# Side work of the attention in a new order, and maxima in two bf16 parts

## The chip, the cores and the metric

One core of one Trainium2 chip runs the whole program in one launch. The metric is the device time in microseconds (us).

## The reference, cut to what matters

The model is two layers on 16 sequences of 512 tokens with 256 features. Layer 0 is a gated convolution mixer and a recurrent network; layer 1 is causal attention and a mixture of experts with a fixed capacity. The change touches only the attention of layer 1:

```python
h = layernorm(x) * (1 + scale_a) + shift_a      # by sequence
q, k, v = split(h @ w_qkv, 3)                   # 16 heads of 16 features; q with a form of head_dirs, head_scales
s = q @ k.T                                     # causal, scaled
p = softmax(s)
x = x + gate_a * ((p @ v) @ w_out)
```

The program folds the scale and the form built from `head_dirs` and `head_scales` into the weight of q ahead of the loop.

## The kernel before, in words

The stages run one after the other: mixer, recurrent network, attention (`attention_stage`), router, choice of the tokens for each expert by counting, experts. The attention stage runs from about 1190 us to 2335 us of the span.

A batch is one sequence (NB = 16, `i` in the code). All five engines have a queue written out by hand, `pe_batch`, `dve_batch`, `act_batch`, the GpSimd block and `sp_batch`, with a loop over the middle batches and the first and last ones unrolled. They are tied by semaphores (`Signal`: `stp(b, k)` is the value after k steps of batch b). Each batch goes over 16 heads in four groups of 4.

**The main work of a head.** q and k are held as three bf16 parts each, in stacks of 96 rows (`q_stack`, `k_stack`), so that one matmul gives a product at nearly fp32 accuracy. `pe_max` (L1221) forms the scores with queries on partitions, seven heads ahead (AHEAD = 7); `dve_max` (L1450, the reduction is L1456) takes the maxima over keys. So head 9 of batch i forms the maxima of head 0 of batch i+1. After each fourth head, `pe_turn_max` (L1299) turns the maxima of the next group into a row, `dve_neg_max` (L1465) splits its negative into three bf16 parts, and `sp_row` (L1716) copies these into rows 96 to 98 of `q_stack`, where `k_stack` holds ones. `pe_scores` (L1240) then forms scores minus maximum with keys on partitions, contracting over 99 rows, `act_exp` (L1576) takes the exponential (L1586), and after four heads `pe_pv` (L1258) multiplies by the values; this product stands in heads 0, 4, 8 and 12. In each head the three fills f = 0, 1, 2 of scores and maxima alternate on TensorE. PSUM banks 0 to 2 hold scores, 3 and 4 maxima, 6 the values product, and 5 and 7 (`SIDE_A`, `SIDE_B`) all side work.

**The side work of batch i,** placed by head:

- head 0: values product of batch i (`pe_values`), kept by ScalarE (`act_values`)
- head 1: turn of the normalised x of batch i+1 (`pe_turn_ln`), then four ScalarE operations (`act_hT`) and two VectorE ones in head 2 (`dve_hT_lo`)
- heads 3 and 4: q and k products of batch i+1 (`pe_qk`, L1292), each of the four results copied to bf16 by ScalarE (`act_qk`, L1618), the rest formed by VectorE (`dve_qk_rest`, L1499), copied again (`act_qk2`, L1622), and the third part formed by GpSimd (`pool_qk3`, L1680)
- heads 2, 6, 9, 13: turns of the product with the values (`pe_turn_o`) and the division (`dve_normal`)
- heads 5, 7 and 8: output projection of batch i-1 (`pe_turn_tok`, `act_o_hi`, `dve_o_lo`, `pe_out`); heads 9 and 10: turning it back and adding it to x
- heads 8 and 11: statistics and normalisation of batch i+2.

**The queue of SyncE** carries all transfers, in the order of the code: `sp_row(i,1)`, `sp_store` of q and of k of batch i+1 to a DRAM buffer (12 transfers), `sp_row(i,2)`, `sp_load` of groups 0 and 1 of batch i+1 (6 transfers each, 768 KB), `sp_row(i,3)`, load 2, `sp_row(i+1,0)`, load 3. A load of group g waits for the scores of group g of batch i, the first one also for the stores:

```python
sp_row(sp, i, 2)
if not last:
    sp_load(sp, i + 1, 0)
    sp_load(sp, i + 1, 1)
```

Of the kernel before, what the change touches and what calls it, by code (L numbers as in the profile page):

```python
# [27 lines left out]
P = 128  # L28
# [1037 lines left out]
STACK = len(Q_PARTS) * HD  # L1066

# [76 lines left out]
def attention_stage(nc, t, ps, mem):  # L1144
# [7 lines left out]
    with ExitStack() as ctx:  # L1152
# [19 lines left out]
        var_eps, rstd = sb("var_eps", [P, TT]), sb("rstd", [P, TT])  # L1172
        xn = sb("xn", [P, TT, D])
# [5 lines left out]
        neg_top = sb("neg_top", [HEADS, 3, P], BF16)  # L1179
        neg_rest = sb("neg_rest", [HEADS, P])  # L1180
# [25 lines left out]
        lnt, hTf, hTh, hTl = signal("ln_turned"), signal("hT_full", DK), signal("hT_hi", DK), signal("hT_lo", DK)  # L1206
        vp, ve = signal("v_product", 2), signal("v_kept", 2)
# [4 lines left out]
        mtp, neg, row = signal("max_turned", NG), signal("neg_max", 4 * NG), [signal(f"max_row{g}", 48) for g in range(NG)]  # L1212
# [27 lines left out]
        def pe_scores(pe, b, h, f, first):  # L1240

            if h % GROUP == 0 and f == 0:
                pe.wait_ge(*row[h // GROUP](b, 48))

            if h:
                pe.wait_ge(*ex(b, 3 * (h - 1) + f + 1))
            elif not first:
                pe.wait_ge(*ex(b - 1, 3 * (HEADS - 1) + f + 1))
            for kt in ((0,), (1, 3), (2,))[f]:
                bk, col = ST_PLACE[kt]  # L1250
                w = T - kt * P
                pe.matmul(bank(bk)[:, col:col + w], k_stack[0:STACK + 3, h, kt * P:(kt + 1) * P],  # L1252
                          q_stack[0:STACK + 3, h, kt * P:T], start=True, stop=True)
                last = pe.matmul(bank(bk)[:, col:col + P], ident_b[:, :], mask_k[:, :],  # L1254
                                 start=False, stop=True, skip_group_check=True)
            last.then_inc(stp.sem, 1)

        def pe_pv(pe, b, g):  # L1258

            pe.wait_ge(*ex(b, 3 * GROUP * (g + 1)))  # L1260
            if g == 0:
                pe.wait_ge(*ve(b, 2))
# [21 lines left out]
        def pe_turn_ln(pe, b):  # L1284
            pe.wait_ge(*s_xn(b, TT))
            for f in range(DK):
                for n in range(TT):
                    last = pe.transpose(bank((SIDE_A, SIDE_B)[f])[:, n * P:(n + 1) * P], xn[:, n, f * P:(f + 1) * P],
                                        ident[:, :])
            last.then_inc(lnt.sem, 1)  # L1290
# [42 lines left out]
        def pe_batch(pe, i, first, last):  # L1333
            for h in range(HEADS):
                for f in range(3):
                    if f == 2 and h % GROUP == 0 and not (first and h == 0):
                        pe.wait_ge(*neg(i, 4 * (h // GROUP + 1)))
                        pe_pv(pe, *((i, h // GROUP - 1) if h else (i - 1, NG - 1)))
# [5 lines left out]
                if h % GROUP == 1 and not (last and h + GROUP > HEADS):  # L1344

                    g = h // GROUP
                    if g:
                        pe.wait_ge(*oe(i, g))
                    else:
                        pe.wait_ge(*(neg(i, 4) if first else oe(i - 1, NG)))  # L1350
                    pe_turn_max(pe, *((i, g + 1) if g + 1 < NG else (i + 1, 0)))
                if h == 0:
                    pe.wait_ge(*(qr(i, 4) if first else on(i - 1, 3)))
                    pe_values(pe, i)
                if h == 1 and not last:
                    pe.wait_ge(*ve(i, 2))
                    pe_turn_ln(pe, i + 1)
                if h == 2 and not first:
                    pe.wait_ge(*(ve(i, 2) if last else hTf(i + 1, 2)))
                    pe_turn_o(pe, i - 1, 3, SIDE_B)  # L1360
                if h == 3 and not last:
                    pe.wait_ge(*hTl(i + 1, DK))
                    pe_qk(pe, 0)
                    if not first:
                        pe.wait_ge(*on(i - 1, NG))
                    pe_qk(pe, 1)
                if h == 4 and not last:
                    for n in range(2):
                        pe.wait_ge(*qr(i + 1, n + 1))
                        pe_qk(pe, 2 + n)  # L1370
                if h == 5 and not first:
                    for f in range(DK):
                        pe.wait_ge(*(ve(i, 2) if last else qr(i + 1, 3 + f)))
                        pe_turn_tok(pe, i - 1, f)
                if h == 6:
                    pe.wait_ge(*(qr(i + 1, 4) if first else yl(i - 1, 2)))
                    pe_turn_o(pe, i, 0, SIDE_B)
                if h == 7 and not first:
# [9 lines left out]
                if h == 10 and not first:  # L1388
# [5 lines left out]
                if h == 14:  # L1394

                    pe.wait_ge(*(on(i, 1) if first else xs(i - 1, 2)))

        @block.tensor
        def _(pe):
            pe_turn_ln(pe, 0)  # L1400
# [3 lines left out]
            for n in range(2):  # L1404
                pe.wait_ge(*qr(0, n + 1))
                pe_qk(pe, 2 + n)
            for h in range(AHEAD):
# [4 lines left out]
            pe_batch(pe, 0, True, False)  # L1412
            with pe.Fori(1, NB - 1) as i:
                pe_batch(pe, i, False, False)
            pe_batch(pe, NB - 1, False, True)
# [25 lines left out]
        def dve_norm(dve, b, first=False):  # L1441
            if not first:
                dve.wait_ge(*lnt(b - 1, 1))
# [15 lines left out]
        def dve_hT_lo(dve, b):  # L1459
            for f in range(DK):  # L1460
                dve.wait_ge(*hTh(b, f + 1))
# [3 lines left out]
        def dve_neg_max(dve, b, g, first=False):  # L1465

            src, k = bank(PV_BANK)[0:HEADS, 0:P], 4 * g
            dve.wait_ge(*mtp(b, g + 1))
            if g or not (first or (isinstance(b, int) and b == 0)):

                dve.wait_ge(*(row[g - 1](b, 48) if g else row[NG - 1](b - 1, 48)))
# [41 lines left out]
        def dve_batch(dve, i, first, last, norm):  # L1513
            for h in range(HEADS):
                if h == 2 and not last:
                    dve_max(dve, i, h + AHEAD, (0, 1))
                    dve_hT_lo(dve, i + 1)
                    dve_max(dve, i, h + AHEAD, (2,))
# [7 lines left out]
                if h == 2 and not first:  # L1526
                    dve_normal(dve, i - 1, 3, SIDE_B)
                if h in (3, 4) and not last:
                    for n in range(2):
                        dve_qk_rest(dve, i + 1, 2 * (h - 3) + n)  # L1530
                if h == 5 and not first:
                    dve_o_lo(dve, i - 1)
                if h == 6:
                    dve_normal(dve, i, 0, SIDE_B)
                if h == 9:
# [3 lines left out]
                if h == 10 and not first:  # L1539
# [3 lines left out]
                if h == 11 and norm:  # L1543
# [5 lines left out]
        def _(dve):  # L1549
# [7 lines left out]
            dve.memset(k_stack[STACK:STACK + 3, :, :], 1.0).then_inc(const.sem, 1)  # L1557
            dve.memset(values[:, :, :, HD:HD + 1], 1.0).then_inc(const.sem, 1)
            dve.memset(values[:, :, :, HD + 1:], 0.0).then_inc(const.sem, 1)
            for h in range(AHEAD):  # L1560
# [33 lines left out]
        def act_values(act, b):  # L1594
            for n in range(2):
                act.wait_ge(*vp(b, n + 1))
                act.activation(values[:, 2 * n:2 * n + 2, :, 0:HD].rearrange("p a h c -> p a h c"),
                               bank((SIDE_A, SIDE_B)[n]).rearrange("p (a h c) -> p a h c", a=2, h=HEADS),
                               ACT.Copy).then_inc(ve.sem, 1)

        def act_hT(act, b):
            act.wait_ge(*lnt(b, 1))
            if not (isinstance(b, int) and b == 0):
                act.wait_ge(*q3(b - 1, 4))
            act.nop(nofuse=True)
            for f in range(DK):
# [3 lines left out]
            for f in range(DK):  # L1610
                act.wait_ge(*hTf(b, f + 1))
                act.activation(hT_s[0][:, f, :], hT[:, f, :], ACT.Copy).then_inc(hTh.sem, 1)

        def act_qk(act, b, n):
            act.wait_ge(*qp(b, n + 1))
            if n == 0 and not (isinstance(b, int) and b == 0):
                act.wait_ge(*stored(b - 1, 32))
# [17 lines left out]
        def act_batch(act, i, first, last):  # L1635
            for h in range(HEADS):
# [3 lines left out]
                if h == 0:  # L1640
                    act_values(act, i)
                if h == 1 and not last:
                    act_hT(act, i + 1)
                if h in (3, 4) and not last:
# [6 lines left out]
                if h in (7, 8) and not first:  # L1651
                    act_delta(act, i - 1, h - 7)

        @block.scalar
        def _(act):
# [6 lines left out]
            act_batch(act, 0, True, False)  # L1662
            with act.Fori(1, NB - 1) as i:
                act_batch(act, i, False, False)
            act_batch(act, NB - 1, False, True)
# [16 lines left out]

        @block.gpsimd
        def _(pool):
# [3 lines left out]
            with pool.Fori(0, NB - 2) as i:  # L1688
                pool_qk3(pool, i + 1)
                pool_rstd(pool, i + 2)  # L1690
            pool_qk3(pool, NB - 1)

# [23 lines left out]
        def sp_row(sp, b, g):  # L1716
            sp.wait_ge(*neg(b, 4 * (g + 1)))
            for j in range(3):
# [861 lines left out]
```

## Time and profile before

| | us |
|---|---|
| median of 3 runs | 2859.42 (2857.22 to 2860.83) |
| the profiled execution, its own time | 2858.73 |
| its span, first to last instruction | 2856.9 |
| TensorE busy | 2382.5 |
| VectorE busy | 1555.3 |
| ScalarE busy | 1290.6 |
| GpSimd busy | 503.2 |
| mean granted TensorE clock | 0.924 of full |

Busy time is summed over the whole span, with stages of different limits. PE is TensorE's matmul queue, PEld its weight loads, DVE VectorE, ACT ScalarE, POOL GpSimd, SP SyncE; a `q` behind a name marks the engine's sequencer. Matmuls overlap and their ends are modelled, so starts are the safer reading. A granted clock of 1.00 is 2.4 GHz and 0.50 is 1.2 GHz. An arrow `<-` behind an idle time names what ended it.

### The profile page before, as it was taken

The numbers are of one execution on the slowest core, as the hardware profiler recorded it, in microseconds if no ns is written. First come the engines' busy times: TensorE is split into PE (matmuls) and PEld (weight loads), VectorE is DVE, ScalarE is ACT, GpSimd is POOL, SyncE is SP. The second block draws the span as 40 slices with busy tenths as digits, with TensorE's granted clock in tenths as the row PEclk, the third lists the DMA queues.
The fourth block names the chain that finished last, engine by engine and source line by source line (L and its number), as shares of the span: only waits on it lengthen the run. The fifth ranks groups of instructions, "written<-read, shape, count | busy, mean of one in ns | idle before, by whom it ended". The sixth has DMA issues, their size and how long they took to land. (4 is left out here: it accounts for less than half of the span.)

```text
span 2856.9 us, 46003 instructions
## 1 busy us (share of the span) xinstructions
PE 2382.5 (83%) x15266; PEld 1797.4 (63%) x15266; DVE 1555.3 (54%) x3568; ACT 1290.6 (45%) x2197; POOL 503.2 (18%) x413
## 2 busy tenths in 40 slices
PE   7999999999699998557888788888888878149997
PEld 6777777777478886435555555555555548139996
DVE  4444444444344443456666666666666556666664
ACT  2444444444355555524555455555555545014442
POOL 0111111111011113400000000000000003026663
PEclk8999999999899999769999999999999989569999
DMA  3200000000100000022233222222222206535542
GB/s 118 77 0 0 0 0 0 0 0 0 30 0 0 0 0 22 24 75 75 69 73 74 70 70 68 67 69 74 69 67 72 71 3 236 157 108 112 124 91 38
DMA packets 123435, 157.38 MB, mean 55 GB/s; under 512 B 26848, under 2 KB 104048, under 8 KB 123248
## 3 DMA queue, kind: packets, MB, share of 16 engines
q1 hardware_dynamic: 109040, 131.17, 16.6%
q0 software_dynamic: 14336, 25.44, 4.6%
q8 instruction: 35, 0.57, 0.1%
q14 instruction: 24, 0.20, 0.0%
HBM read 96.78 MB, written 58.98 MB: 55 GB/s over the span
## 5 line engine op out<-in xcount | busy, mean ns | idle before, releaser
L1456 DVE TENSOR_REDUCE at_top<-psum 128x1 f32<-128x512 f32 (+3 forms) x1024 | 448.0, 484 | 334.7 <-PE psum L1236 331.8
L1586 ACT ACTIVATE at_probs<-psum 128x512 f32<-128x512 f32 (+1 forms) x768 | 372.1, 530 | 407.5 <-PE psum L1254 405.2
L1234 PE MATMUL psum<-at_k_stack,at_q_stack 96*128 96x512 bf16 (+3 forms) x1024 | 299.7, 319 | 167.0 <-DMA at_k_stack<-qk_parts 116.9
L1252 PE MATMUL psum<-at_q_stack,at_k_stack 99*128 99x512 bf16 (+3 forms) x1024 | 293.0, 313 | 40.8 <-DMA at_q_stack<-at_neg_top 24.2
L1234 PEld LDWEIGHTS psum<-at_k_stack,at_q_stack 96*128 96x128 bf16 x1024 | 104.4, 102 | 271.2 <-issue 100.4
L1236 PE MATMUL psum<-at_mask_q,at_ident_b 128*128 128x128 bf16 x1024 | 208.1, 229 | 0.0
L1254 PE MATMUL psum<-at_mask_k,at_ident_b 128*128 128x128 bf16 x1024 | 204.7, 226 | 0.0
L1252 PEld LDWEIGHTS psum<-at_q_stack,at_k_stack 99*128 99x128 bf16 x1024 | 103.8, 101 | 135.8 <-issue 62.1
L1680 POOL TENSOR_TENSOR at_q_parts<-at_hT,at_q_parts 128x512 bf16<-128x512 f32 x32 | 36.6, 1165 | 681.3 <-ACT at_q_parts L1622 681.3
L1270 PE MATMUL psum<-at_probs,at_values 128*32 128x512 f32 (+3 forms) x2048 | 151.8, 437 | 0.9 <-ACT at_probs L1586 0.9
L570 POOL TENSOR_TENSOR y<-y,mean 128x512 f32<-128x512 f32 x64 | 83.3, 1330 | 366.0 <-ACT mean L623 366.0
L2288 POOL DMA_INDIRECT out<-ex_result,slot_tokens x64 | 119.9, 1874 | 101.9 <-DVE ex_result L2420 87.3
L613 ACT ACTIVATE y_hi<-y 128x512 fp32r<-128x512 f32 x64 | 40.5, 632 | 164.6 <-DVE y L491 164.6
L2466 ACT ACTIVATE ex_mid<-psum,ex_b_up 128x512 f32<-128x512 f32 x96 | 66.2, 689 | 107.0 <-PE psum L61 103.6
L1270 PEld LDWEIGHTS psum<-at_probs,at_values 128*32 128x32 f32 x2048 | 60.1, 110 | 82.4 <-issue 63.7
L59 PE MATMUL psum<-ex_w_down_hi,ex_mid_hi 128*128 128x256 f32 x384 | 109.0, 284 | 1.4 <-DVE ex_mid_lo L2399 1.4
L61 PE MATMUL psum<-ex_w_down_hi,ex_mid_lo 128*128 128x256 f32 x384 | 107.5, 280 | 0.0
L60 PE MATMUL psum<-ex_w_down_lo,ex_mid_hi 128*128 128x256 f32 x384 | 107.5, 280 | 0.0
L1254 PEld LDWEIGHTS psum<-at_mask_k,at_ident_b 128*128 128x128 bf16 x1024 | 104.2, 102 | 1.8
L1236 PEld LDWEIGHTS psum<-at_mask_q,at_ident_b 128*128 128x128 bf16 x1024 | 105.1, 103 | 0.0
L59 PE MATMUL psum<-hT_hi,w_in_hi 128*128 128x512 f32 x256 | 102.0, 398 | 3.5 <-DVE hT_lo L426 3.5
L59 PE MATMUL psum<-h_hi,w_conv_hi 128*128 128x512 f32 x256 | 102.4, 400 | 0.0
(405 smaller groups left out, 6215.1 us busy)
## 6 DMA issues: line engine op xcount, KB each, us to landing
qk_parts<-at_q_parts SPq DMA_DIRECT2D x96, 128.0 KB
qk_parts<-at_k_parts SPq DMA_DIRECT2D x96, 128.0 KB
at_q_stack<-qk_parts SPq DMA_DIRECT2D x64, 192.0 KB
at_k_stack<-qk_parts SPq DMA_DIRECT2D x64, 192.0 KB
x_residual<-in_x SPq DMA_DIRECT2D x16, 512.0 KB, 8.5
at_q_stack<-qk_parts SPq DMA_DIRECT2D x64, 128.0 KB
at_k_stack<-qk_parts SPq DMA_DIRECT2D x64, 128.0 KB
token_rows<-ro_h_tok SPq DMA_DIRECT2D x16, 512.0 KB, 3.1
```

The source lines that it names most:

```text
L59: pe.matmul(out, w[0], x[0], start=start, stop=False)
L60: pe.matmul(out, w[0], x[1], start=False, stop=False)
L61: return pe.matmul(out, w[1], x[0], start=False, stop=stop)
L570: pool.tensor_tensor(dev[:, m, :], y[:, m, :], mean[:, :], ALU.subtract).then_inc(dv.sem, 1)
L1234: pe.matmul(out, q_stack[0:STACK, h, qt * P:(qt + 1) * P], k_stack[0:STACK, h, 0:w], start=True, stop=True)
L1236: last = pe.matmul(bank(MAX0 + n % 2)[:, col + w - P:col + w], ident_b[:, :], mask_q[:, :], start=False, stop=True, skip_group_check=True)
L1252: pe.matmul(bank(bk)[:, col:col + w], k_stack[0:STACK + 3, h, kt * P:(kt + 1) * P], q_stack[0:STACK + 3, h, kt * P:T], start=True, stop=True)
L1254: last = pe.matmul(bank(bk)[:, col:col + P], ident_b[:, :], mask_k[:, :], start=False, stop=True, skip_group_check=True)
L1270: last = pe.matmul(bank(PV_BANK)[32 * hh:32 * hh + 32, kt * P:T], values[:, kt, GROUP * g + hh, :], probs[:, slot(GROUP * g + hh), P_COL[k ...
L1456: dve.tensor_reduce(top[:, h, qt:qt + 1], bank(MAX0 + n % 2)[:, col:col + w], AX.X, ALU.max).then_inc(mxr.sem, 1)
L1586: act.activation(probs[:, slot(h), 512 * f:512 * f + w], bank(f)[:, 0:w], ACT.Exp).then_inc(ex.sem, 1)
L2288: pool.indirect_dma_start(out=rows_out, out_offset=bass.IndirectOffsetOnAxis(ap=index[:, e, c * TT + a:c * TT + a + 1], axis=0), in_=resul ...
```

## The change

- The maxima are split into two bf16 parts instead of three (`N_SHIFT = 2`): two VectorE operations and one of the three row transfers per group are gone, and the scores contract over 98 rows.
- The q and k products of batch i+1 and all that follows from them stand in heads 0 and 1.
- The turn of the normalised x is for batch i+2, one half in head 13 and the other in head 14, half f = 1 first; ScalarE's four operations stand in head 14, VectorE's two in head 15.
- The values product is that of batch i+1, in head 3. ScalarE keeps it as it lies in a new tile `v_tok`, and GpSimd copies that into `values`, 32 columns a head (`pool_values`).
- Turns and divisions of the product with the values are in heads 4, 7, 10 and 13; the output projection in heads 5 to 9, with its second product behind head 9 instead of head 8; its way back in heads 10 and 11; the normalisation in head 12.
- Ahead of batch 0 the values of batch 0 and the normalised x of batch 1 are made as well. One more batch (the last but one) is unrolled on TensorE, ScalarE and GpSimd.
- The queue of SyncE keeps its order.

```diff
+N_SHIFT = 2
...
-        neg_top = sb("neg_top", [HEADS, 3, P], BF16)
-        neg_rest = sb("neg_rest", [HEADS, P])
+        neg_top = sb("neg_top", [HEADS, N_SHIFT, P], BF16)
...
+                if h in (0, 1) and not last:
+                    for n in (2 * h, 2 * h + 1):
+                        if n == 0:
+                            pe.wait_ge(*hTl(i + 1, DK))
+                        elif n >= 2:
+                            pe.wait_ge(*qr(i + 1, n - 1))
+                        pe_qk(pe, n)
+                if h == 3 and not last:
+                    pe.wait_ge(*qr(i + 1, 4))
+                    pe_values(pe, i + 1)
+                if h == 4 and not first:
+                    if not last:
+                        pe.wait_ge(*ve(i + 1, 2))
                     pe_turn_o(pe, i - 1, 3, SIDE_B)
-                if h == 3 and not last:
-                    pe.wait_ge(*hTl(i + 1, DK))
-                    pe_qk(pe, 0)
...
-                if h == 8 and not first:
-                    pe.wait_ge(*on(i, 1))
-                    pe_out(pe, i - 1, 1)
                 if h == 9:
-                    pe.wait_ge(*(qr(i + 1, 3) if first else dl(i - 1, 1)))
+                    if not first:
+                        pe.wait_ge(*on(i, 1))
+                        pe_out(pe, i - 1, 1)
...
                 if h == 13:
                     pe.wait_ge(*on(i, 2))
                     pe_turn_o(pe, i, 2, SIDE_A)
...
+                    if turn:
+                        pe.wait_ge(*(on(i, 1) if first else xs(i - 1, 2)))
+                        pe_turn_ln(pe, i + 2, 1)
+                if h == 14 and turn:
+                    pe.wait_ge(*on(i, 3))
+                    pe_turn_ln(pe, i + 2, 0)
...
             dve.wait_ge(*neg(b, k + 1))
-            dve.scalar_tensor_tensor(neg_rest[:, :], src, -1.0, neg_top[:, 0, :], ALU.mult,
+            dve.scalar_tensor_tensor(neg_top[:, 1, :], src, -1.0, neg_top[:, 0, :], ALU.mult,
                                      ALU.subtract).then_inc(neg.sem, 1)
-            dve.wait_ge(*neg(b, k + 2))
-            dve.tensor_copy(neg_top[:, 1, :], neg_rest[:, :]).then_inc(neg.sem, 1)
-            dve.wait_ge(*neg(b, k + 3))
-            dve.tensor_tensor(neg_top[:, 2, :], neg_rest[:, :], neg_top[:, 1, :], ALU.subtract).then_inc(neg.sem, 1)
...
+                if h in (0, 1) and not last:
+                    for n in range(2):
+                        dve_qk_rest(dve, i + 1, 2 * h + n)
+                if h == 4 and not first:
                     dve_normal(dve, i - 1, 3, SIDE_B)
...
-                if h == 5 and not first:
+                if h == 6 and not first:
                     dve_o_lo(dve, i - 1)
...
+                if h in (0, 1) and not last:
                     for n in range(2):
-                        act_qk(act, i + 1, 2 * (h - 3) + n)
+                        act_qk(act, i + 1, 2 * h + n)
                     for n in range(2):
-                        act_qk2(act, i + 1, 2 * (h - 3) + n)
-                if h == 5 and not first:
+                        act_qk2(act, i + 1, 2 * h + n)
+                if h == 3 and not last:
+                    act_values(act, i + 1)
+                if h == 6 and not first:
                     act_o_hi(act, i - 1)
...
+                if h == 14 and turn:
+                    act_hT(act, i + 2)
...
+        def pool_values(pool, b):
+            pool.wait_ge(*ve(b, 2))
+            if isinstance(b, int) and b == 0:
+                pool.wait_ge(const.sem, 3)
+            else:
+                pool.wait_ge(*pv(b - 1, NG))
+            pool.nop(nofuse=True)
+            pool.tensor_copy(values[:, :, :, 0:HD], v_tok[:, :, :].rearrange("p a (h c) -> p a h c", h=HEADS)
+                             ).then_inc(vs.sem, 1)
...
         def sp_row(sp, b, g):
-            sp.wait_ge(*neg(b, 4 * (g + 1)))
-            for j in range(3):
+            sp.wait_ge(*neg(b, N_SHIFT * (g + 1)))
+            for j in range(N_SHIFT):
```

## Rows read from the trace of the kernel before

**Rows 1.** The page, part 1: busy us, share of the span, instructions.
```profile
PE 2382.5 (83%) x15266; PEld 1797.4 (63%) x15266; DVE 1555.3 (54%) x3568; ACT 1290.6 (45%) x2197; POOL 503.2 (18%) x413
```

**Rows 2.** Windows: stretch, its us, busy us by engine, granted clock, DMA share, GB/s.
```profile
1390.01:1458.56 68.55, 56.86 (x488) 37.36 (x489) 43.00 (x112) 35.23 (x70) 5.56 (x5) 0.95 0.27 70
1436.70:1443.50 6.80, 5.26 (x26) 3.96 (x27) 3.78 (x11) 1.12 (x3) 0.00 (x0) 0.50 0.14 57
1290.00:1293.40 3.40, 3.40 (x20) 1.53 (x22) 1.45 (x3) 1.19 (x2) 0.00 (x0) 0.50 0.24 75
...
1452.00:1457.00 5.00, 3.95 (x37) 2.54 (x36) 4.86 (x14) 3.12 (x8) 0.00 (x0) 1.00 0.28 60
1457.00:1459.00 2.00, 1.76 (x17) 1.06 (x16) 1.79 (x5) 1.23 (x3) 0.00 (x0) 1.00 0.01 2
```

**Rows 3.** TensorE's waits, 1325 to 2277 us: us in total, times, longest.
```profile
PE psum L1234 <- DMA at_k_stack<-qk_parts: 86.2, 14, 6.7
PE psum L1234 <- DVE at_top L1456: 40.4, 57, 1.0
PE psum L1252 <- DMA at_q_stack<-at_neg_top: 15.2, 15, 1.4
PE psum L1252 <- ACT at_probs L1586: 15.0, 26, 0.9
```

**Rows 4.** Timeline of TensorE in one batch: start, us, instruction, idle before it.
```profile
1408.12 0.39 PE L1252 MATMUL psum<-at_q_stack,at_k_stack 99*128 99x512 bf16 x1
...
1409.46 2.36 PE L1270 MATMUL psum<-at_probs,at_values 128*32 128x512 f32 x32
1412.07 0.48 PE L59 MATMUL psum<-at_hT_hi,at_wk_hi 128*128 128x512 f32 x1
...
1414.95 0.39 PE L1252 MATMUL psum<-at_q_stack,at_k_stack 99*128 99x512 bf16 x1
...
1426.38 0.39 PE L1252 MATMUL psum<-at_q_stack,at_k_stack 99*128 99x512 bf16 x1 [1.39 <-DMA at_q_stack<-at_neg_top]
...
1431.79 0.39 PE L1252 MATMUL psum<-at_q_stack,at_k_stack 99*128 99x512 bf16 x1
...
1438.24 0.61 PE L1234 MATMUL psum<-at_k_stack,at_q_stack 96*128 96x512 bf16 x1 [6.00 <-DMA at_k_stack<-qk_parts]
```

**Rows 5.** Timeline of SyncE, which issues the transfers, same batch.
```profile
1418.63 3.63 SPq L1701 DMA_DIRECT2D qk_parts<-at_k_parts  x6
1422.38 1.83 SPq L1719 DMA_DIRECT2D at_q_stack<-at_neg_top  x3
1425.75 1.97 SPq L1713 DMA_DIRECT2D at_q_stack<-qk_parts  x3
...
1429.31 1.85 SPq L1713 DMA_DIRECT2D at_q_stack<-qk_parts  x3
...
1446.79 1.92 SPq L1713 DMA_DIRECT2D at_q_stack<-qk_parts  x3
```

**Rows 6.** Timeline of VectorE: a rest, and pieces two and four of the maxima.
```profile
1414.38 0.69 DVE L1499 TENSOR_TENSOR at_hT<-psum,at_k_parts 128x512 f32<-128x512 f32 x1 [1.65 <-ACT at_k_parts L1618]
...
1418.28 0.28 DVE L1474 SCALAR_TENSOR_TENSOR at_neg_rest<-psum,at_neg_top 16x128 f32<-16x128 f32 x1
...
1418.84 0.28 DVE L1479 TENSOR_TENSOR at_neg_top<-at_neg_rest,at_neg_top 16x128 bf16<-16x128 f32 x1
```

**Rows 7.** Timeline of TensorE in batch 0: the waits for a transfer.
```profile
1289.71 0.39 PE L1252 MATMUL psum<-at_q_stack,at_k_stack 99*128 99x512 bf16 x1 [3.38 <-DMA at_q_stack<-at_neg_top]
1301.47 0.61 PE L1234 MATMUL psum<-at_k_stack,at_q_stack 96*128 96x512 bf16 x1 [5.76 <-DMA at_k_stack<-qk_parts]
```

**Rows 8.** Groups of GpSimd, 1190 to 2330 us: busy us, mean ns, idle before.
```profile
L1680 POOL TENSOR_TENSOR at_q_parts<-at_hT,at_q_parts 128x512 bf16<-128x512 f32 x32 | 36.6, 1165 | 681.3 <-ACT at_q_parts L1622 681.3
```

**Rows 9.** Groups of ScalarE, same stretch and columns.
```profile
L1618 ACT ACTIVATE at_k_parts<-psum 128x512 bf16<-128x512 f32 x32 | 19.1, 597 | 24.2 <-PE psum L61 24.2
```

More of the change, by code:

```diff
@@ L1211, in attention_stage @@
         mxp, mxr = signal("max_scores", 3 * HEADS), signal("max", 4 * HEADS)
-        mtp, neg, row = signal("max_turned", NG), signal("neg_max", 4 * NG), [signal(f"max_row{g}", 48) for g in range(NG)]
+        mtp, neg, row = signal("max_turned", NG), signal("neg_max", N_SHIFT * NG), [signal(f"max_row{g}", 16 * N_SHIFT) for g in range(NG)]
         stp, ex = signal("scores", 3 * HEADS), signal("exp", 3 * HEADS)
@@ L1282, in pe_values, with pe_turn_ln @@
                 last.then_inc(vp.sem, 1)
-        def pe_turn_ln(pe, b):
+        def pe_turn_ln(pe, b, f):
             pe.wait_ge(*s_xn(b, TT))
[L1286 to L1289, printed above, removed]
+            for n in range(TT):
+                last = pe.transpose(bank((SIDE_A, SIDE_B)[f])[:, n * P:(n + 1) * P], xn[:, n, f * P:(f + 1) * P],
+                                    ident[:, :])
             last.then_inc(lnt.sem, 1)
@@ L1330, in pe_turn_delta, with pe_batch @@
             last.then_inc(hp.sem, 1)
-        def pe_batch(pe, i, first, last):
+        def pe_batch(pe, i, first, last, turn):
             for h in range(HEADS):
@@ L1349, in pe_batch @@
                     else:
-                        pe.wait_ge(*(neg(i, 4) if first else oe(i - 1, NG)))
+                        pe.wait_ge(*(neg(i, N_SHIFT) if first else oe(i - 1, NG)))
                     pe_turn_max(pe, *((i, g + 1) if g + 1 < NG else (i + 1, 0)))
[L1352 to L1357, printed above, removed]
@@ L1385, in pe_batch @@
+                if h == 10:
+                    pe.wait_ge(*(ve(i + 1, 2) if first else dl(i - 1, 1)))
                     pe_turn_o(pe, i, 1, SIDE_A)
@@ L1387, in pe_batch @@
                         pe_turn_delta(pe, i - 1, 0)
-                if h == 10 and not first:
+                if h == 11 and not first:
                     pe.wait_ge(*xs(i - 1, 1))
@@ L1459, in dve_hT_lo @@
         def dve_hT_lo(dve, b):
-            for f in range(DK):
-                dve.wait_ge(*hTh(b, f + 1))
+            for k, f in enumerate((1, 0)):
+                dve.wait_ge(*hTh(b, k + 1))
                 dve.tensor_tensor(hT_s[1][:, f, :], hT[:, f, :], hT_s[0][:, f, :].bitcast(F32),
@@ L1514, in dve_batch @@
             for h in range(HEADS):
[L1515 to L1518, printed above, removed]
+                if h == 15 and norm:
+                    dve_max(dve, i + 1, h + AHEAD - HEADS, (0, 1))
+                    dve_hT_lo(dve, i + 2)
+                    dve_max(dve, i + 1, h + AHEAD - HEADS, (2,))
                 elif h + AHEAD < HEADS:
@@ L1538, in dve_batch @@
                         dve_add(dve, i - 1, 0)
-                if h == 10 and not first:
+                if h == 11 and not first:
                     dve_add(dve, i - 1, 1)
@@ L1609, in act_hT @@
                                scale=mod[:, SCALE_A + f, bass.ds(b, 1)]).then_inc(hTf.sem, 1)
-            for f in range(DK):
-                act.wait_ge(*hTf(b, f + 1))
+            for k, f in enumerate((1, 0)):
+                act.wait_ge(*hTf(b, k + 1))
+                if k == 0 and not (isinstance(b, int) and b == 0):
+                    act.wait_ge(*vp(b - 1, 2))
                 act.activation(hT_s[0][:, f, :], hT[:, f, :], ACT.Copy).then_inc(hTh.sem, 1)
@@ L1633, in act_delta, with act_batch @@
                            scale=mod[:, GATE_A + m, bass.ds(b, 1)]).then_inc(dl.sem, 1)
-        def act_batch(act, i, first, last):
+        def act_batch(act, i, first, last, turn):
             for h in range(HEADS):
@@ L1661, in _ @@
                     act_qk2(act, 0, 2 * m + n)
[L1662 to L1665, printed above, removed]
+            act_values(act, 0)
+            act_hT(act, 1)
+            act_batch(act, 0, True, False, True)
+            with act.Fori(1, NB - 2) as i:
+                act_batch(act, i, False, False, True)
+            act_batch(act, NB - 2, False, False, False)
+            act_batch(act, NB - 1, False, True, False)
             b = NB - 1
```

105 lines of the change are left out of this document (50 added, 55 removed).

## The prediction

> **What bounds the kernel now.** I began with the page's engine totals: TensorE is busy 83% of the span and no other engine over 54% [rows 1]. The page's chain that ended last stays in the last stage, so it says nothing about attention. I therefore took one steady batch of the attention by itself, from the first score product of one batch to that of the next: 68.55 us, TensorE busy 56.86, VectorE 43.00, ScalarE 35.23, GpSimd 5.56 [rows 2]. So TensorE sets the pace and is idle 11.7 us a batch. The list of TensorE's waits over the 14 steady batches (1 to 14) says for what [rows 3]: 86.2/14 = 6.16 us a batch for the loads of the next batch's q and k stacks, 15.2/14 = 1.09 us for the row of negated maxima, 40.4/14 = 2.89 us for the maxima on VectorE, 15.0/14 = 1.07 us for the exponentials on ScalarE. In the timeline of the batch that starts at 1390 the big wait stands in one place: 6.00 us before the first maximum of the next batch, in head 9, and 1.39 us of row wait before head 8 [rows 4]. Right behind the big wait the granted clock is 0.50, the 1.2 GHz level, for 6.8 us [rows 2].
>
> The timeline of SyncE shows why the loads are late [rows 5]. The store of k is issued from 1418.63 to 1422.26, then the three row transfers, then load 0 at 1425.75, and load 1 at 1429.31. TensorE gets load 0 at 1438.24, 12.5 us after its first issue [rows 4, 5]. The queue runs in the order of the code: sp_row(i,1), two stores, sp_row(i,2), loads 0 and 1. The row was ready when VectorE ended its fourth piece at 1419.12 [rows 6], but queued behind the store.
>
> **The change part by part.** I count heads by their first score product: head 5 starts at 1414.95, head 8 at 1426.38 after its wait, head 9 at 1431.79 [rows 4].
>
> *Row wait.* The q and k products move from heads 3 and 4 to heads 0 and 1, three heads earlier. The stores then end before head 5's maxima are turned. The row for head 8 is no longer behind them: it is ready at head 5 + 3.6 us (below) and lands some 2 us after issue (head 5 + 7), whereas head 8 starts at head 5 + 10. The 1.09 us goes.
>
> *Load wait.* Load 0 still stands behind sp_row(i,2), which needs the maxima of head 5. So it moves forward only to: second VectorE piece ended at 1418.28 + 0.28 = 1418.56, head 5 + 3.6 [rows 6]; two row issues instead of three, 2 x 0.61 = 1.2 [rows 5]; 0.2 for hand-over (estimate). First load issue at head 5 + 5.0, against + 10.8 before. Do the stores hold it up? The k store's last issue was at 1422.26 and load 0 started 3.5 us later, at 1425.75, the moment the store had landed [rows 5]: head 4 + 17.6, with head 4 at 1408.12 [rows 4]. The new head 1 has no probabilities-by-values product in it (about 2 us; 2.36 with its modelled end [rows 4]), so k has landed at about head 1 + 15.6, and head 5 + 5.0 is head 1 + 21. There are 5 us to spare.
>
> When does it land? Load 1 follows at once, since it only waits for the scores of head 7; so the nearest row is the 12.5 us of the same pair: head 5 + 17.5. When does TensorE want it? Head 9 came 16.84 us after head 5. Off go 1.39 of row wait and one output product, which moves behind head 9: 12 such matmuls took from 1412.07 to 1414.95, so 6 take 1.4 [rows 4]. That leaves 14.05, and 0.45 for the first scores: head 5 + 14.5. New wait 3.0 us; gain 6.16 - 3.0 = 3.2. The bound below: load 2 alone, issued at 1446.79, has no traffic left after 1457 [rows 2, 5], 10.2 us, which makes the wait 0.6. The bound above is the present 6.2.
>
> The Trainium skill, page "DMA: Bandwidth & Descriptors", section "Rules for kernel authors", says that a copy whose outermost dimension is a broadcast of c copies uses at most c of the 16 DMA engines; the loads of q repeat a part 3 and 2 times that way. This trace agrees: a load's tail runs at a DMA share of 0.28 and 0.14 [rows 2]. By that rule two loads in a row share the same few engines and the second one lengthens the first, which speaks against rival B and for the 12.5 us: 2780 by the rule, 2733 without it.
>
> *Clock.* After the 6 us wait the engine does 5.26 us of busy work at 0.50 [rows 2]; at full clock that is half, so 2.6 us a batch are lost. The only gap near 3 us in this stage that began at full clock, 3.38 us before 1289.71, was followed by a stretch of 3.40 us at 0.50 [rows 2, 7], which costs 1.7. The new gap is a little shorter and its place in time will vary, so I take half of that, 0.85, and a gain of 1.8. Bounds: 0 (nothing gained) to 2.6.
> The Trainium skill, "TensorE: Matmul & The Clock Gate", section "What's actually happening", says the clock follows how busy the engine has recently been. By that rule a gap left in head 9 can still drop the clock and give 0 here; rival C prices this from the rows.
>
> *New small waits.* Now 4.0 us a batch go on waits for VectorE and ScalarE, for the most part just behind the q and k side work, which queues in front of maxima and exponentials [rows 3]. Before, the second half of it sat in head 4 with its values product, about 2 us of TensorE work that hides the chain ScalarE copy, VectorE rest, ScalarE copy. Head 1 has none. VectorE can't take head 1's maxima until two 0.6 us copies and 0.69 us rests of head 0 are done [rows 6, 9], about 1.3 us into head 1, so TensorE waits some 0.9 at its third fill; the same in head 2 and at head 3's first exponential (0.9 together); ScalarE's four operations on the normalised x now stand between the exponentials of heads 14 and 15 (1.1, as now in head 2); the o_lo pair moves to the bare head 6 and holds the maxima of head 7 (1.4); 0.7 stays in heads 10 and 11. Sum 5.0. The two VectorE pieces fewer are off the path except in the load's chain, counted above. I take +1.1 net. Bounds: -1 (all in slack) to +11, rival D. The places are read from the code's order, the sizes are estimates from these durations.
>
> *Costed at nothing.* GpSimd's new spreading copy of the values: its subtraction over 512 elements takes 1.16 us [rows 8], so 1024 elements take some 2.3 us; it starts after head 0's values product and GpSimd next has work 4 us later. Cover gone, it delays q's third part and the stores, which have 5 us to spare. The score product contracts over 98 rows instead of 99: same duration by columns. ScalarE's copy of the values keeps its size. More code (one more unrolled batch): nothing in the trace prices it; I take 0, up to 10 us in all.
>
> *Sum of a steady batch:* -1.1 -3.2 -1.8 +1.1 = -5.0 us; times 14 = -70.
>
> *Batch 0 and the start.* Batch 0 waited 3.38 and 5.76 us [rows 7]. It has no output product or token turn between heads 5 and 9 (1.4 + 0.85), so its new load wait is 3.0 + 2.25 = 5.3: gain 3.9. Its clock drop shortens by 1.7, the new waits cost 1.1: about -4. Before it, the first values product (24 matmuls of half width, 2.8 us) and the last batches' turn (0.9) fall into the first load's long wait or away, and the wait for the first row loses two VectorE pieces and one issue, 1.1: about -5.
>
> Total -79 us. The profiled span is 2856.9 and its own time 2858.7, 0.7 under the median; 2856.9 - 79 = 2778, plus 1.8 = 2780.
>
> **The rivals.**
> *A, as above:* load wait about 3 us: 2780, own range 2765 to 2800. Chance 0.48.
> *B, the load comes in time:* it takes 10.2 us, the wait is 0.6, and the clock doesn't fall: -1.1 -5.6 -2.6 +1.1 = -8.2, x14 = -115, less 11 at the start: 2733. For it: load 2 alone. Against: load 1 is issued right behind. 0.20.
> *C, the wait shrinks but the clock falls all the same:* -1.1 -3.2 +1.1 = -3.2, x14 = -45, -9: 2805. For it: the 3.38 us gap that dropped the clock. 0.17. In its extreme the small waits take up the load wait's gain as well and the change gives nothing measurable (2859): 0.05.
> *D, slower:* the side work stops TensorE in heads without a values product. Ceiling, with nothing overlapped: 16 ScalarE operations of 0.60 (9.6) and 8 VectorE ones of 0.69 (5.5) are 15.1 us of waits against 4.0 [rows 3, 6, 9]: +11.1 -6.1 = +5.0 a batch, x14 = +70, -9: 2920. It decides from waits of about 10.7 us a batch on. Against: today the same chains cost 4.0. 0.10.
>
> **How the numbers follow.** A and most of B and C hold 0.85; the range 2730 to 2835 leaves out D, the no-gain case and a little of B. About 0.2% (6 us) is what a measurement here can tell from no change. Faster 0.85, same 0.05, slower 0.10.
>
> **What would show it.** The steady period falls from 68.3 to about 63.3. The wait on the row before head 8 is gone. Load 0's first issue comes 5 us after head 5, no longer right behind a store, and the wait in head 9 is 2.5 to 3.5 us. The 0.50 stretches are shorter or fewer. TensorE's waits for maxima and exponentials rise to about 5 us a batch, in heads 1, 2 and 7. Wrong would be: a load wait under 1 us or near 6, waits over 8 us in the bare heads, or rows that still queue behind stores.

## The result, and the profile after

The changed kernel takes 2777.48 us, the median of 4 runs (2776.81 to 2780.32), against 2858.38 for the kernel before in 4 runs: a ratio of 0.972, 95% interval 0.9706 to 0.9735. The forecast was 2780, range 2730 to 2835. The profiled span went from 2856.9 to 2778.2 us, 78.7 less, of which 76.4 lie in the attention stage.

TensorE's waits over batches 1 to 14, the list that answers to [rows 3]; us in total, times, longest:

```profile
PE psum L1235 <- DMA at_k_stack<-qk_parts: 47.2, 14, 3.9
PE psum L1235 <- DVE at_top L1461: 46.3, 70, 1.0
PE psum L1253 <- ACT at_probs L1588: 15.7, 27, 1.1
PE psum L1253 <- DMA at_q_stack<-at_neg_top: 0.8, 2, 0.6
```

The load wait (the first line; the view names the transfer of a load that was issued last) is 47.2/14 = 3.37 us a batch instead of 6.16, the row wait 0.06 instead of 1.09. The waits for maxima and exponentials rose from 3.96 to 4.43.

One steady batch and the stretch behind its load wait, as windows (columns as in [rows 2]):

```profile
1442.57:1507.05 64.48, 56.56 (x488) 37.36 (x489) 41.03 (x104) 34.73 (x71) 6.60 (x6) 0.95 0.31 74
...
1483.50:1489.90 6.40, 6.36 (x26) 4.17 (x27) 2.24 (x6) 1.74 (x4) 0.00 (x0) 0.50 0.11 44
```

The same batch on TensorE: heads 5 and 9, and the end of the load wait, as in [rows 4]:

```profile
1466.55 0.38 PE L1253 MATMUL psum<-at_q_stack,at_k_stack 98*128 98x512 bf16 x1
...
1479.92 0.39 PE L1253 MATMUL psum<-at_q_stack,at_k_stack 98*128 98x512 bf16 x1
...
1483.54 0.61 PE L1235 MATMUL psum<-at_k_stack,at_q_stack 96*128 96x512 bf16 x1 [3.17 <-DMA at_k_stack<-qk_parts]
```

SyncE in that batch, as in [rows 5]:

```profile
1458.52 3.88 SPq L1725 DMA_DIRECT2D qk_parts<-at_k_parts  x6
1469.67 1.21 SPq L1743 DMA_DIRECT2D at_q_stack<-at_neg_top  x2
1471.08 1.97 SPq L1737 DMA_DIRECT2D at_q_stack<-qk_parts  x3
...
1474.62 1.85 SPq L1737 DMA_DIRECT2D at_q_stack<-qk_parts  x3
```

The k store is issued by 1462.4, and SyncE then stands still until the row of head 5's maxima is ready at 1469.67. Load 0 starts at 1471.08, head 5 + 4.5 us (it was + 10.5), and TensorE has it at 1483.54, 12.5 us later. The order of the queue is now what holds the load back, where before it was the store: by the traces' semaphore events the last transfer of the store had landed 0.02 us before load 0 was issued in the kernel before, and 5.1 us before it in the changed one (batches 2 to 4). The clock still falls: to 0.50 for 3.4 or 6.8 us in 13 of the 14 batches.

### The profile page after: what moved, and what is told of

Same layout as the page of the kernel before. It is cut to its first block and busy times, and to the rows that moved or that the text cites. A ratio compares the mean times of both kernels' runs of the same rounds, so it can differ in the third digit from the quotient of the medians.

```text
span 2778.2 us, 45597 instructions
## 1 busy us (share of the span) xinstructions
PE 2366.8 (85%) x15266; PEld 1791.3 (64%) x15266; DVE 1525.3 (55%) x3440; ACT 1282.9 (46%) x2197; POOL 518.5 (19%) x429
## 5 line engine op out<-in xcount | busy, mean ns | idle before, releaser
L1588 ACT ACTIVATE at_probs<-psum 128x512 f32<-128x512 f32 (+1 forms) x768 | 365.8, 530 | 346.5 <-PE psum L1255 344.5
L1253 PE MATMUL psum<-at_q_stack,at_k_stack 98*128 98x512 bf16 (+3 forms) x1024 | 288.9, 309 | 23.1 <-ACT at_probs L1588 16.8
L1253 PEld LDWEIGHTS psum<-at_q_stack,at_k_stack 98*128 98x128 bf16 x1024 | 102.5, 100 | 115.1 <-issue 44.2
L61 PE MATMUL psum<-hT_hi,w_in_lo 128*128 128x512 f32 x256 | 102.0, 398 | 0.0
```

The lines of the kernel that those rows point to most:

```text
L61: return pe.matmul(out, w[1], x[0], start=False, stop=stop)
L1253: pe.matmul(bank(bk)[:, col:col + w], k_stack[0:STACK + N_SHIFT, h, kt * P:(kt + 1) * P], q_stack[0:STACK + N_SHIFT, h, kt * P:T], start=T ...
L1588: act.activation(probs[:, slot(h), 512 * f:512 * f + w], bank(f)[:, 0:w], ACT.Exp).then_inc(ex.sem, 1)
```

## The experiments

Every run is timed against the kernel before on the same chip. Unless its diff says otherwise it starts from the changed kernel. "First use" is the matmul that ends or would end the load wait; means over batches 2 to 12, and the period over batches 1 to 13, all worked out from the traces:

| run | us | ratio (95%) | period | load 0 issued, after head 5 | issue to first use | load wait |
|---|---|---|---|---|---|---|
| before | 2858 | | 68.36 | 10.46 | 12.66 | 6.13 |
| changed | 2777.5 | 0.972 (0.9706-0.9735) | 63.69 | 4.53 | 12.56 | 3.28 |
| e1 load first | 2799.1 | 0.979 (0.9777-0.9810) | 64.85 | -0.36 | no wait | 0 |
| e2 two parts alone | 2849.5 | 0.997 (0.9956-0.9981) | 68.10 | 10.46 | 12.70 | 6.38 |
| e3 three parts | 2804.3 | 0.982 (0.9799-0.9831) | 65.33 | 5.72 | 12.63 | 4.54 |
| e4 load 1 later | 2804.0 | 0.981 (0.9791-0.9824) | 65.30 | 4.53 | 11.13 | 1.85 |
| e5 row from ScalarE | 2781.6 | 0.974 (0.9719-0.9752) | 63.92 | -0.54 | no wait | 0 |
| e6 the same, before | 2857.1 | 1.000 (0.9990-1.0009) | 68.42 | 10.50 | 12.61 | 7.34 |
| e7 single loads | 2691.7 | 0.942 (0.9406-0.9437) | 58.61 | 4.53 | no wait | 0 |
| e8 single, first | 2698.6 | 0.945 (0.9429-0.9461) | 58.76 | -0.43 | no wait | 0 |
| e9 single, before | 2754.8 | 0.964 (0.9622-0.9654) | 62.01 | 10.48 | 7.41 | 0.90 |
| e10 cut by heads | 2732.1 | 0.956 (0.9542-0.9574) | 60.61 | 4.53 | 10.94 | 1.65 |
| e11 single, three parts | 2704.9 | 0.946 (0.9445-0.9476) | 59.16 | 5.72 | no wait | 0 |

**Which half of the change did it: e2 and e3.** e2 gives the kernel before the two parts alone:

```diff
-            dve.scalar_tensor_tensor(neg_rest[:, :], src, -1.0, neg_top[:, 0, :], ALU.mult,
+            dve.scalar_tensor_tensor(neg_top[:, 1, :], src, -1.0, neg_top[:, 0, :], ALU.mult,
                                      ALU.subtract).then_inc(neg.sem, 1)
-            dve.wait_ge(*neg(b, k + 2))
-            dve.tensor_copy(neg_top[:, 1, :], neg_rest[:, :]).then_inc(neg.sem, 1)
-            dve.wait_ge(*neg(b, k + 3))
-            dve.tensor_tensor(neg_top[:, 2, :], neg_rest[:, :], neg_top[:, 1, :], ALU.subtract).then_inc(neg.sem, 1)
...
-            for j in range(3):
+            for j in range(2):
```

> The kernel before, with the maxima in two parts and nothing else changed. Theory (before, load 0 started when the stores had landed, so a shorter row does not move it): load 0 still starts at head 4 + 17.6 us, the row wait of head 8 shrinks by up to 0.6 us and the load wait of head 9 grows by as much; the time is within 3 us of before. Rival (the two parts carry a share of the gain by themselves): 10 us or more faster.

It came out 8.7 us faster, more than the 3 expected and less than the rival's 10. The steady period fell by only 0.26 us, 3.4 over 13 batches; the attention stage as a whole took 4.8 us less, and 3.8 of the difference between the two profiled executions lies ahead of the stage, in code that is the same. The place of load 0 did not move.

e3 starts from the changed kernel and makes the maxima three parts again.

> The changed kernel, with the maxima in three parts again. Theory (in the new order load 0 does stand behind the row): two VectorE pieces and one issue, together 1.2 us, are back ahead of load 0, its wait goes from 3.4 to about 4.5 us, the low stretches of the clock are 6.8 us in nearly every batch, the steady period is about 65.3 us and the time about 2801 us. Rival (the order alone gave everything): 2778 us.

As forecast in three points: 1.19 us later issue, load wait 4.54, 2804 us. The fourth was missed: the low stretches of the clock are 3.4 us in 10 of the 14 batches and 6.8 in only four, so a longer wait did not make the clock dearer. The order alone is worth 54 us, the two parts alone at most 9, and together they give 81, so the two parts are worth 27 us in the new order. Of the 1.64 us a batch that they save there, 1.2 are load wait, since they stand in front of the late load; the rest is nearly all waits for maxima, 0.5 of them in head 14.

**Is it the place in the queue: e1, e5 and e6.** e1:

```diff
-            sp_row(sp, i, 2)
             if not last:
                 sp_load(sp, i + 1, 0)
+            sp_row(sp, i, 2)
+            if not last:
                 sp_load(sp, i + 1, 1)
```

> The changed kernel, with load 0 of the next batch put ahead of the row transfers of group 2 in the queue of SyncE. Theory (what is left of the load wait is load 0 standing behind the row, which needs the maxima of head 5): load 0 starts when the k store has landed, about 0.8 us before head 5 instead of 4.5 us after it, lands 12.5 us later, before head 9 asks for it; the 3.4 us wait goes, the granted clock stays at 1.00 through the batch, the steady period falls from 63.6 to about 59 us and the kernel to about 2711 us. Rival (the load is held by the transfers themselves, and gets longer or starts no sooner): a wait of 2 us or more stays in head 9 and the time stays above 2750 us.

A miss: 22 us slower than the changed kernel. The load wait did go. TensorE at head 8 and then SyncE in one batch of this run:

```profile
1547.84 0.61 PE L1253 MATMUL psum<-at_q_stack,at_k_stack 98*128 98x512 bf16 x1 [4.14 <-DMA at_q_stack<-at_neg_top]
```

```profile
1534.86 1.94 SPq L1737 DMA_DIRECT2D at_q_stack<-qk_parts  x3
1536.85 1.34 SPq L1737 DMA_DIRECT2D at_k_stack<-qk_parts  x3
1538.70 1.21 SPq L1743 DMA_DIRECT2D at_q_stack<-at_neg_top  x2
```

Load 0 starts before head 5 as forecast, and the row is issued only a little late, at 1538.70. But the scores of head 8 wait for it until 1547.84: 9 us for 8 KB, in two transfers of 4 KB. The row wait is 56.4/14 = 4.03 us a batch, more than the 3.37 of load wait that went. The view of that line has all four rows of a batch together: typical 1.7 us, the longest 8.6. The two transfers of this row took 3.8 to 4.3 and 7.5 to 8.6 us.

```profile
DMA to landing us min/median/max: 1.7/1.7/8.6
```

So neither theory held as it was put: the wait changed its object. e5 tries the row on another queue (load 0 ahead of it as in e1, `sp_row(sp, i, 2)` gone):

```diff
+        def act_row(act, b, g):
+            act.wait_ge(*neg(b, N_SHIFT * (g + 1)))
+            for j in range(N_SHIFT):
+                act.dma_start(q_stack[STACK + j:STACK + j + 1, GROUP * g:GROUP * (g + 1), :].rearrange(
+                    "a h (q p) -> a (h q) p", p=P), neg_top[:, j, :]).then_inc(row[g].sem, 16)
...
+                if h == 6:
+                    act_row(act, i, 2)
```

> The changed kernel, with load 0 as soon as the k store has landed, and the row transfers of group 2 issued by ScalarE in head 6, on a queue of their own. Theory (in the run with load 0 ahead of the row, the row of 8 KB sat 4 to 8 us behind the load's data in the same queue): from its own queue it lands about 2 us after its issue, head 8 waits under 1 us, the load wait of head 9 is gone and the clock stays at 1.00: steady period about 59.3 us, time about 2716 us. Rival (the row waits for the load's data on the transfer engines, whatever queue it comes from): 3 to 4 us of wait stay in head 8 and the time stays near 2799 us.

Its own queue did not free the row. Landing times of that line:

```profile
DMA to landing us min/median/max: 2.2/4.1/6.3
```

The row wait of head 8 fell to 20.3/13 = 1.56 us, but ScalarE is held for the issues, the two o_hi operations come later and with them VectorE's o_lo, and head 7 waits 2.0 us for maxima instead of 0.9. In the end the run is 4 us over the changed kernel, although its listed waits are 0.7 us a batch shorter (7.2 against 7.9). The difference is the clock, which the theory had at 1.00: behind the waits in heads 7 and 8 it fell in all 14 batches, for 6.8 us in 10 of them. A window inside such a stretch:

```profile
1545.00:1548.00 3.00, 3.00 (x19) 1.10 (x21) 1.14 (x3) 0.60 (x1) 0.00 (x0) 0.50 0.13 52
```

The rival was right on the mechanism, a wait on the transfer engines whatever queue, and wrong on the size.

e6 is the same edit (three parts, no change of the loads) on the kernel before:

> The kernel before, with the row transfers of group 2 issued by ScalarE in head 6 and nothing else changed. Theory (before, load 0 waited for the stores of the products of heads 3 and 4, not for the row): load 0 still starts at head 4 + 17.6 us; the row wait of head 8 shrinks, the load wait of head 9 grows by as much, and the time is within 5 us of 2858. Rival (it was the row in the queue that held up the loads before, too): 20 us or more faster.

Ratio 1.000. The row wait is gone (1.4 us in all in the list, against 15.2 before) and the load wait grew from 6.13 to 7.34. Load 0 is still issued at head 5 + 10.5 with no row in front of it: before, it was the store alone that held it.

**Why a load takes 12.5 us: e4, e7, e10.** e4 puts `sp_load(sp, i + 1, 1)` behind `sp_row(sp, i, 3)`.

> The changed kernel, with load 1 moved behind the row of group 3, so that load 0 has the transfer engines to itself. Theory (the second load lengthens the first): TensorE gets load 0 about 10 us after its first issue instead of 12.5, the wait in head 9 falls to about 1 us and the clock stays up there; but load 1 is then late for head 13 and about as much is lost there. Rival (a load takes 12.5 us by itself): the wait in head 9 stays at 3.4 us, and the wait in head 13 comes on top.

Issue to use fell to 11.1 us, not 10; the wait in head 9 to 1.85; and 3.9 us of wait appeared in head 13, where load 1 is wanted. So the second load costs the first one 1.4 us. The clock did not stay up as expected, it fell in every batch, and the run is 26 us slower than the changed kernel. e7 cuts the loads:

```diff
-                sp.dma_start((q_stack, k_stack)[side][n[0] * HD:n[1] * HD, GROUP * g:GROUP * (g + 1), :], src
-                             ).then_inc(loaded[g].sem, 16)
+                for s in range(n[1] - n[0]):
+                    sp.dma_start((q_stack, k_stack)[side][(n[0] + s) * HD:(n[0] + s + 1) * HD,
+                                                          GROUP * g:GROUP * (g + 1), :], src[s]
+                                 ).then_inc(loaded[g].sem, 16)
...
-        loaded = [signal(f"loaded{g}", 16 * len(LOADS)) for g in range(NG)]
+        loaded = [signal(f"loaded{g}", 16 * sum(n[1] - n[0] for _, n, _ in LOADS)) for g in range(NG)]
```

> The changed kernel, with each load of a group cut into 12 transfers of one part each (16 partitions, 64 KB) instead of 6 that have the repeated or stacked parts as their outermost dimension; the same bytes. Theory (a load takes long because two of its large transfers run on 3 or 2 of the 16 engines): the DMA share in a load rises, load 0 is there about 9 us after its first issue instead of 12.5, most of it 12 issues of 0.5 to 0.6 us, and the 3.4 us wait in head 9 goes: steady period about 59.5 us, time about 2720 us. Rival (a load is bound by its bytes or by the issues): 12 us or more, the wait stays at 3 us or grows.

2691.7 us, 86 us under the changed kernel and 28 under the theory's 2720, which had the load there in 9 us and the period at 59.5, and is no more than the gain of 14 such batches; the way to batch 0 alone is 6.8 us shorter. SyncE at load 0 in one batch, and windows of load 0 and of a whole batch:

```profile
1506.36 2.72 SPq L1738 DMA_DIRECT2D at_q_stack<-qk_parts  x6
1509.12 2.73 SPq L1738 DMA_DIRECT2D at_k_stack<-qk_parts  x6
```

```profile
1506.40:1513.80 7.40, 6.37 (x71) 3.62 (x69) 5.52 (x14) 3.71 (x9) 0.00 (x0) 1.00 0.44 125
...
1477.79:1536.40 58.61, 53.78 (x489) 35.64 (x489) 40.88 (x104) 34.39 (x71) 6.60 (x6) 1.00 0.28 81
```

A single transfer is issued in 0.46 us. In the changed kernel the two copies of q that repeat a part take 0.84 and 0.71, the other four 0.46 each, so twice as many transfers cost 5.5 us instead of 3.4. Each lands 2.3 us after its issue, the last one of load 0 7.4 us after the first. The DMA share is 0.44 over the load and no lower at its end; in the changed kernel it falls to 0.18 in the last 3 us before TensorE has load 0 and to 0.11 in the tail of load 1.

The semaphore events of the traces say which copies make this tail. The twelve transfers of a load raise its semaphore in 192 steps, 16 each. The six of the changed kernel do it in 71: 16 each for four of them and 7 for two, with one early step right behind the issue of each of the first two, which are the copies of q that repeat a part. e10, where four transfers repeat a part, has 142 steps, four of them early. This points to these two, three and two times the same part, as the ones that run on few engines; the copies of k with three and two parts stacked have the issue time and the number of steps of the single ones. That it would be enough to cut these two is argued from the events; no run cuts them alone.

The steady batch has no wait for a transfer and a granted clock of 1.00 throughout. TensorE's waits in the steady batches, all there are:

```profile
PE psum L1235 <- DVE at_top L1461: 45.0, 68, 1.0
PE psum L1253 <- ACT at_probs L1588: 15.5, 26, 1.1
```

e10 makes as many transfers of the same bytes, but cut between pairs of heads, so that the outermost dimension keeps its 3 or 2 parts:

```diff
+                for c in range(2):
+                    a = GROUP * g + 2 * c
+                    sp.dma_start((q_stack, k_stack)[side][n[0] * HD:n[1] * HD, a:a + 2, :], src[:, :, 2 * c:2 * c + 2, :]
+                                 ).then_inc(loaded[g].sem, 16)
```

> The changed kernel, with each load in 12 transfers as in the run e7, but cut between two pairs of heads, so that the outermost dimension keeps its 3, 2 or 1 parts; the same bytes and the same number of transfers as e7. Theory (what counts is how many transfer engines a transfer is spread over): the load is as slow as in the changed kernel or slower by the six more issues, the wait in head 9 is 3 to 6 us, time 2775 to 2815 us. Rival (more and smaller transfers are faster by their number): as e7, about 2692 us.

It lies between the two, 2732 us; neither the theory's numbers nor the rival's came out. Issue to use is 10.9 us, like the 11.1 of e4: with 6.6 us of issues the second load starts 6.7 us behind the first instead of 3.5, so load 0 is nearly alone. That this is all of e10's gain is argued, not shown. What is left to e7, 10.9 against 7.4 us with the same number of transfers and the same bytes, comes from the form of the transfers: 1.1 us of it is issue time, the rest the tail, which here still has a DMA share of 0.19.

**What order and parts are worth once loads are short: e8, e9, e11.** e8 is e7 and e1 together.

> Both: loads in 12 single transfers, and load 0 ahead of the row of group 2. Theory: the load's data are spread over all engines and gone before the row is issued, so the row lands within 3 us of its issue, no wait is left in heads 8 and 9, the clock stays at 1.00: steady period about 59 us, time about 2712 us. Rival (any load ahead of the row delays it by its data, spread or not): 2 us or more of wait in head 8.

The waits came out as the theory had them, none from batch 4 on, but nothing is gained over e7 either: 7 us more. From batch 4 on the period is the same, 58.6 us; batches 0 and 1 wait 1.5 and 1.2 us for the row. The two profiled executions are 4.1 us apart: 2.9 of it has come up by the start of batch 15, and 1.7 comes in that batch. e9 is the edit of e7 on the kernel before.

> The kernel before, with each load of a group in 12 single transfers (16 partitions each) as in the run e7, and nothing else changed. Theory (the new order is worth what the lateness of load 0 costs; with a load that is there 7.4 us after its first issue, load 0 comes about 1 us late even in the old order): load 0 still starts behind the stores and the row, its wait falls from 6.2 to about 1 us, the row wait of 1.1 us stays, the clock stays at 1.00: steady period about 60.5 us, time about 2742 us. Rival (the order is worth its 81 us whatever the loads take): 2772 us or more, 81 us over the run e7.

The load wait is 11.8/13 = 0.91 us and the row wait 13.7/13 = 1.05, as forecast:

```profile
PE psum L1234 <- DVE at_top L1456: 51.0, 65, 1.1
PE psum L1252 <- ACT at_probs L1586: 14.3, 26, 0.9
PE psum L1252 <- DMA at_q_stack<-at_neg_top: 13.7, 13, 1.4
PE psum L1234 <- DMA at_k_stack<-qk_parts: 11.8, 13, 1.1
```

The time is 2755, 13 over the forecast, since a wait for maxima of 1.05 us came up in head 10 that the big wait had covered. The loads alone are thus worth 104 us in the old order, more than the whole change; the whole change (order and parts) is worth 81 us with the long loads and 63 with the short ones, 2754.8 - 2691.7 (from two chips, on which the kernel before is 1.9 us apart). e11 is e7 with three parts.

> The changed kernel with single loads as in the run e7, and with the maxima in three parts. Theory (two parts are worth 27 us in the new order only because they stand ahead of a late load 0): with fast loads the 1.2 us more ahead of load 0 are in slack, only small waits for VectorE grow by up to 0.5 us a batch: 2692 to 2702 us. Rival (the two pieces and the transfer have a price of their own): 2715 us or more.

2704.9, 3 us outside the range given: 0.55 us more a batch over batches 1 to 13, of which 0.41 are small waits (4.92 against 4.51). These batches make 7 of the 13 us; the way to batch 0, that batch and the last two make 3.6. The two parts keep a little under half of their 27 us.

## Why the prediction was right, point by point

**The load wait** held in place and size: issue at head 5 + 4.5 (forecast 5.0), 12.56 us to the first use (12.5), head 9 at head 5 + 13.4 (14.05), wait 3.3 (3.0). The load and head 9 both came earlier than forecast, by 0.5 and 0.7 us, so most of the two errors cancelled. In batch 0 the wait was 6.8 us, not 5.3. The step "load 0 still stands behind sp_row(i,2)" is shown by e3, where 1.19 us more ahead of the load became 1.26 us more wait. That the store was the cause before is shown by e6 and e2, and by its landing 0.02 us before the issue of load 0; the 5 us to spare of the new order were 5.1. (By its own terms rival B's wait is 5.0 + 10.2 - 14.5 = 0.7, not 0.6.)

**The row wait** went, as forecast: 1.09 us a batch to 0.06.

**The clock** was mis-sized. Without the listed waits, from start to start of its matmuls, TensorE needs 57.1 us a batch in the kernel before and 55.0 in e9, whose clock stays at 1.00 in the same order; 55.8 in the changed kernel and 54.1 in e7. So the low stretches cost 2.1 us a batch before and 1.7 after, a gain of 0.4 where I had put 1.8. A wait half as long drops the clock nearly as often, since waits of 2.8 to 3.9 us are still enough in 13 of 14 batches; the shortest, 2.79 us, is the one that left it up. In e10, with waits of 1.1 to 2.7 us, it stayed up in 11 of 14. On this point rival C was right: the row of the 3.38 us gap [rows 7] said it, and I took only half of it.

**The new small waits** were mis-sized the other way: +0.5 us a batch instead of +1.1. They came where they were expected: heads 1 and 2, 0.6 each (0.9 and 0.9 expected with head 3, which has 0.2), head 7 0.9 (1.4), head 0 1.0 (1.1); and one in head 13, 1.0, was there in head 14 before. A further 0.9 us was gained that no step names: between e9 and e7 the time from start to start falls by 0.93 us a batch, with the same matmuls and the listed waits left out. It lies mostly at the first matmuls of and behind the turns of the maxima and of the product with the values, and behind the output product. It is not idle time too short for the list: gaps under 0.15 us make 0.3 us a batch in both. So it stands under the modelled ends of the matmuls ahead; what it waits for there, and why the new order shortens it, stays open.

**The sum of a steady batch** was -5.0 and is -4.67: load -2.85, row -1.1, clock -0.4, listed small waits +0.5, unlisted -0.9, which makes -4.7. That the sum came within 0.3 us is partly luck: the clock gave 1.4 less than forecast, the small waits cost 0.6 less, and 0.9 came from a place that the prediction does not have.

**The ends.** The way to batch 0 was to gain 5 us and gained 0.7. The values product did move into the long wait, but the saving shows only in batch 15, which no longer has it and is 4.5 us shorter; the prediction counted it at the start. The wait for the first row stayed, 5.4 us: the second transfer of that row took 3.8 us to land behind the loads, which is e1's mechanism. Batch 0 gained 5.1 (forecast 4), in spite of its longer load wait.

**At nothing.** GpSimd's copy took 1.04 us, not 2.3, and delayed nothing:

```profile
L1698 POOL COPY at_values<-at_v_tok x16: 1038/1040/1291, 1219.6 to 2208.8; 128x1024 f32<-128x1024 f32 x16
```

**The form of the loads** was used in the prediction only to keep rival B small. e7 and e9 show that it is worth more than the whole change, 86 us in the new order and 104 in the old: the 12.5 us that the sum takes as given are a matter of the transfer's form.

## What to carry to other kernels

When a stall waits for a transfer, follow that transfer both ways: what stands before it in its queue (here the store before, the row after the change; an edit in front of it pays only while it is the last of the two), and why it takes as long as it does. A tail with a low DMA share is a sign that a copy runs on few engines; cutting the copies so that their outermost dimension was the 16 partitions of a part gave more here than the whole new order. A stall that was halved, from 6.2 to 3.4 us, gave its own length back but next to nothing of the clock; at 1.1 to 2.7 us (e10) most of the clock was back too. In e5, with 2.0 us in one head and 0.9 to 2.3 in the next, it was not.

## What the runs showed of the hardware that was not expected

- A 4 KB transfer of the row that lands 1.7 us after its issue when no load is under way took up to 8.6 us behind 768 KB issued just before on the same queue (e1), and up to 6.3 us when it came from another engine's queue (e5).
- With the loads in single transfers the same order costs the row next to nothing: in e8 its transfers land in 1.7 to 2.0 us behind the load, and from batch 4 on head 8 does not wait.
- A copy with three or two parts stacked in its source (k) took no longer to issue than a single one, 0.46 us, and made as many semaphore steps, 16; the copies that repeat one part (q) took 0.84 and 0.71 us and made seven together.
- Waits of TensorE of 2.8 to 3.9 us were followed by a clock of 1.2 GHz for 3.4 or 6.8 us in 13 of 14 batches, while waits of 0.91 us and 1.05 us in one batch (e9) left it at 2.4 GHz. A wait of 2.0 us in head 7 with one of 0.9 to 2.3 us in head 8 (e5) was followed by 1.2 GHz in all 14 batches.
